# Long tiles: 2 to 4 key blocks of each unit's probabilities turned by DMA instead of by TensorE

## The reference, cut to what matters

```
x = x + attn(layernorm(x))        # 16 heads, key of 64 + 64 numbers a token, value of 128
x = x + ffn(layernorm(x))         # 16 experts of 176, the best 2 a token, and a shared one of 352

q = (h @ Wqa @ Wqb)               # 16 heads x (64 without, 64 with rotation)
c_kv, k_pe = split(h @ Wkva)      # 64 + 64 numbers a token, shared by all heads
scores = q_full . k_full * 128 ** -0.5, causal
probs  = softmax(scores)
out    = (probs @ v) @ Wo         # v = c_kv @ Wkvb[v part]
```

## Time and profile before

| | |
|---|---|
| median of 3 runs | 1752.13 us (1750.12 to 1752.58) |
| the profiled execution | 1753.84 us, its span 1752.0 us |
| PE busy | 1522.4 us (87%) |
| DVE busy | 1308.7 us (75%) |
| ACT busy | 1027.3 us (59%) |
| POOL busy | 990.5 us (57%) |
| transposes of probabilities on PE (L838) | 2304 |
| granted TensorE clock, mean | 0.971 |

### The profile page before, as it was taken

The page is one execution under the profiler, slowest core; times in us unless marked ns, Lnnn a source line. Parts: engine busy times, 40 slices in busy tenths (PEclk is TensorE's granted clock), DMA queues, the critical chain, the costliest instruction groups (busy, mean ns, idle before and its releaser), DMA issues.

```text
span 1752.0 us, 45002 instructions
## 1 busy us (share of the span) xinstructions
PE 1522.4 (87%) x16388; PEld 1092.0 (62%) x16389; DVE 1308.7 (75%) x2967; ACT 1027.3 (59%) x2342; POOL 990.5 (57%) x1597
## 2 busy tenths in 40 slices
PE   8777988989879999998799999987999999889990
PEld 2355666666646776666477766664676676666660
DVE  2676888888768778887687788776877888655556
ACT  1365656656546666666566666664666666556660
POOL 3156774436477667456776765567776443553440
PEclk9989999999999999999999999999999999999995
DMA  6236752221353332213534332135232311347418
GB/s 179 55 87 140 153 78 42 60 55 35 69 98 65 69 65 60 54 28 67 109 64 69 62 63 54 21 66 117 62 66 54 59 27 30 87 131 225 136 42 292
DMA packets 329877, 144.41 MB, mean 82 GB/s; under 512 B 277346, under 2 KB 320389, under 8 KB 329672
## 3 DMA queue, kind: packets, MB, share of 16 engines
q1 hardware_dynamic: 304592, 105.41, 30.1%
q10 hardware_dynamic: 18168, 19.41, 3.6%
q0 software_dynamic: 6912, 16.83, 3.0%
HBM read 47.04 MB, written 29.53 MB: 44 GB/s over the span
## 4 chain that ended last, share of the span: by engine, by line
PE 48%; DVE 26%; ACT 9%; issue 6%; DMA 4%; SPq 3%; POOL 1%; ACTq 0%; DVEq 0%; POOLq 0%
PE of_ps L677 20%; PE s_ps L677 16%; PE t_ps L838 10%; DVE pT L1609 7%; DVE smax L1580 3%; ACT pT L1024 3%; DVE smax L1584 2%; DVE smax L1562 1%; SPq L467 1%; ACT probs L1151 1%; DVE nmax L1588 1%; DVE nmax L1591 1%; ACT probs L1156 1%; ACT work L1024 1%; DVE work L1414 1%
## 5 line engine op out<-in xcount | busy, mean ns | idle before, releaser
L1609 DVE TENSOR_TENSOR pT<-t_ps,pT 128x512 f16<-128x512 f32 (+3 forms) x688 | 409.6, 598 | 194.3 <-ACT pT L1024 190.9
L677 PE MATMUL s_ps<-kT,qT 128*128 128x512 f16 (+3 forms) x2304 | 493.3, 329 | 11.3 <-DMA qT<-work 6.7
L1024 ACT CAST pT<-t_ps 128x512 f16<-128x512 f32 (+3 forms) x688 | 354.5, 515 | 233.6 <-PE t_ps L838 232.9
L838 PE MATMUL t_ps<-id,probs 128*128 128x128 f32 x2304 | 383.3, 281 | 71.2 <-DVE pT L1609 31.5
L838 PEld LDWEIGHTS t_ps<-id,probs 128*128 128x128 f32 x2304 | 258.8, 142 | 176.5 <-issue 91.6
L1151 ACT ACTIVATE probs<-s_ps,nmax,fac 128x640 f32<-128x640 f32 (+3 forms) x256 | 269.0, 1051 | 1.7 <-DVE nmax L1588 1.7
L677 PEld LDWEIGHTS s_ps<-kT,qT 128*128 128x128 f16 x2304 | 219.4, 99 | 79.5 <-DMA qT<-work 7.2
L677 PEld LDWEIGHTS of_ps<-ckv,pT 128*128 128x128 f16 x6912 | 240.6, 98 | 37.5 <-DVE o_sb L1443 7.6
L677 PE MATMUL of_ps<-ckv,pT 128*128 128x64 f16 x6912 | 257.9, 193 | 5.5 <-DVE o_sb L1443 5.2
L677 PE MATMUL of_ps<-weights,xT 128*128 128x512 f16 (+1 forms) x936 | 208.5, 361 | 59.8 <-ACT work L1024 30.5
L1887 POOL TENSOR_TENSOR os_<-o_sb,os_ 128x512 f16<-128x512 f32 x60 | 70.2, 1169 | 178.0 <-ACT os_ L1024 175.7
(11 more groups left out here) (224 smaller groups left out, 2472.3 us busy)
## 6 DMA issues: line engine op xcount, KB each, us to landing
wgu_sb<-wgu ACTq DMA_DIRECT2D x8, 704.0 KB, 4.3
work<-lists SPq DMA_DIRECT2D x40, 128.5 KB, 2.1
qT<-lists SPq DMA_DIRECT2D x40, 128.5 KB, 2.1
x_sb<-x SPq DMA_DIRECT2D x32, 128.0 KB, 2.4
x<-x SPq DMA_DIRECT2D x32, 128.0 KB, 2.4
dense<-den SPq DMA_DIRECT2D x32, 128.0 KB
weights<-dense ACTq DMA_DIRECT2D x1, 4096.0 KB, 20.0
qT<-y_exp SPq DMA_DIRECT2D x16, 256.0 KB, 6.6
```

What stands on the lines that cost most here:

```text
L677: return pe_.matmul(o, a, b, start=start, stop=stop)
L838: last = pe_.transpose(t_ps[:, h, c * P:(c + 1) * P], probs[:, u % 2, g * L + j * P:g * L + (j + 1) * P], id32[:, :])
L1024: return act.copy(o, i)
L1609: dve.tensor_tensor(pT[:, u % 2, 1, h, 0:w], t_ps[:, h, 0:w], pT[:, u % 2, 0, h, 0:w], ALU.subtract).then_inc(s.lo_p, 1)
```

## The change

In the four long tiles the first d = 2, 3, 3, 4 key blocks of a unit (i = 4, 5, 6, 7) are no longer turned by PE. ACT casts them from `probs` to a staging area that lies just ahead of `probs` (high part), DVE writes the low part over the start of `probs` itself, and one DMA transposes both, 2 d blocks, into `pT`. PE turns the other 3, 3, 4, 4 blocks, in one piece, through the bank u % 2 of `t_ps`. The number of ACT and DVE instructions for it stays two each a unit. `values` takes the PE part first.

New waits: the exponentials of unit k + 2 (and DVE's shifted write) wait until the DMA has read unit k; a DMA waits for DVE's low part and for the values of two units before; the values wait for the DMA. PE's turn waits for the low part of the last unit in the same bank, two units before. On ACT the order in iteration k becomes exps(k+1), prob_hi(k), staged_hi(k+1), on DVE the maxima of k+2, prob_lo(k), staged_lo(k+1).

On the SP queue a unit's transposition stands at the start of each iteration, and the other DMAs of a long tile are given places between them. The queries' transposition becomes four pieces of 8 blocks: two at the end of the tile, two after the first two units of the next (all four at its end for i = 7). The x2T, xT and store of tile 3 move into tile 4.

Also: the low part of the first output half of tile 1 goes ahead of the normalized rows on POOL, and its DMA ahead of keys and queries; `q0` of tile 2 moves from (1, 3) to (2, 0); the shared expert's result is added into `x1` and stored from there, without the buffer `den`.

```diff
+TURNED = [0, 0, 0, 0, 2, 3, 3, 4]
+def queries_in(n):
+    return 16 * sum(4 if m >= 2 and TURNED[(m - 2) % TB] else 1 for m in range(n % 2, n + 1, 2))
+def halves_by_pe():
+    uses, last = {}, {}
+    for t, u in units_in_order():
+        dma = TURNED[t % TB] > 0
+        for h in (1,) if dma else (0, 1):
+            bank = u % 2 if dma else h
+            uses[t, u, h] = (len(uses), bank, last.get(bank))
+            last[bank] = len(uses) - 1
+    return uses
...
-        probs = sb("probs", [P, 2, S], F32)
-        pT = sb("pT", [P, 2, 2, 2, 512], F16)
+        STAGE = 2 * P
+        probs_mem = sb("probs_mem", [P, 2, STAGE + S], F32)
+        probs = probs_mem[:, :, STAGE:]
+        pT = sb("pT", [P, 2, 2, 1024], F16)
...
+            def turn_query_part(n, part):
+                if part == 0:
+                    sp.wait_ge(s.rope_done, n + 1)
...
+                a, hs_ = part // 2, slice(part % 2 * 8, part % 2 * 8 + 8)
+                sp.dma_start_transpose(qT[:, n % 2, a, part % 2 * 8 * P:(part % 2 + 1) * 8 * P].rearrange("p (h n) -> p h n", n=P),
+                                       qs_of(n)[:, a, hs_, :].rearrange("p h d -> p (h d)")).then_inc(q_in[n % 2], 16)
+            def turn_probs(t, u):
+                g_ = unit_of(t, u)
+                sp.wait_ge(s.lo_s, DMA_UNIT[t, u] + 1)
+                sp.wait_ge(s.pv_made, g_ - 1)
+                d = TURNED[t % TB]
+                sp.dma_start_transpose(pT[:, u % 2, 0, 0:2 * d * P].rearrange("p (k n) -> p k n", n=P),
+                                       probs_mem[:, u % 2, :].bitcast(F16)[:, 2 * STAGE - d * P:2 * STAGE + d * P]).then_inc(p_in[u % 2], 16)
...
+            def long_section(t):
+                n, p, q, m = t + 2, t - 1, t - 2, t + 4
+                i = t % TB
+                for k in range(units(t)):
+                    turn_probs(t, k)
+                    if i == 4:
+                        if k == 0:
+                            turn_x2(p - 1)
+                        if k == 1 and has(m - 1):
+                            turn_x(m - 1)
+                        if k == 2:
+                            store_dense(q - 1)
+                    elif k < 2 and has(n - 1):
+                        turn_query_part(n - 1, k + 2)
+                    if k == 3:
+                        load_residual(p)
+                    if k == 4:
+                        turn_output(p, 1)
+                    if k == 5 and has(m + 1):
+                        load_x(m + 1)
+                    if k == 9:
+                        turn_hidden(q)
+                    if k == 12 and i < 7 and n % TB > 0 and has(n):
+                        turn_keys(n)
+                    if k == 13:
+                        turn_x2(p)
+                    if k == 14 and has(m):
+                        turn_x(m)
+                    if k == 14 and i == 7 and has(t + 1):
+                        turn_keys(t + 1)
+                        turn_keys(n)
+                    if k == 15:
+                        turn_output(t, 0)
+                        store_dense(q)
+                if has(n):
+                    for part in range(4 if i == 7 else 2):
+                        turn_query_part(n, part)
...
+            d = TURNED[i]
+            if d:
+                return [(0, j) for j in (range(d, i + 1) if h else range(d))]
...
                 pe_.wait_ge(s.exp_done, 2 * g_ + h + 1)
-                if g_ > 0:
-                    pe_.wait_ge(s.lo_p, 2 * (g_ - 1) + h + 1)
+                if before is not None:
+                    pe_.wait_ge(s.lo_p, before + 1)
...
-                for h in range(2):
-                    pe_.wait_ge(s.lo_p, 2 * g_ + h + 1)
+                order = (1, 0) if by_dma(t, u) else (0, 1)
+                for h in order:
+                    if (t, u, h) in PE_HALF:
+                        pe_.wait_ge(s.lo_p, PE_HALF[t, u, h][0] + 1)
+                    else:
+                        pe_.wait_ge(p_in[u % 2], 16 * (DMA_UNIT[t, u] // 2 + 1))
...
                 if h == 0:
                     act.wait_ge(s.max_ready, g_ + 1)
+                    staged_free(act, t, u)
...
+            def staged_hi(t, u):
+                act.wait_ge(s.exp_done, 2 * unit_of(t, u) + 2)
+                copy(staged(t, u, 0), probs[:, u % 2, 0:P * TURNED[t % TB]]).then_inc(s.hi_s, 1)
...
                     exps_ahead(t, k, 0)
                     prob_hi(t, k, 1)
+                    ahead = unit_of(t, k) + 1
+                    if ahead < len(UNIT_AT) and by_dma(*UNIT_AT[ahead]):
+                        staged_hi(*UNIT_AT[ahead])
...
+            def staged_lo(t, u):
+                dve.wait_ge(s.hi_s, DMA_UNIT[t, u] + 1)
+                dve.tensor_tensor(staged(t, u, 1), probs[:, u % 2, 0:P * TURNED[t % TB]], staged(t, u, 0),
+                                  ALU.subtract).then_inc(s.lo_s, 1)
```

More of the change, by code:

```diff
@@ L78, in shares_rope, with units_in_order, units_by_dma @@
     return n < 2 or n % TB in (2, 3)
+TURNED = [0, 0, 0, 0, 2, 3, 3, 4]
+def queries_in(n):
+    return 16 * sum(4 if m >= 2 and TURNED[(m - 2) % TB] else 1 for m in range(n % 2, n + 1, 2))
+def units_in_order():
+    return [(t, u) for t in range(NT) for u in range(units(t))]
+def halves_by_pe():
[7 more added lines that the diff above has]
+    return uses
+def units_by_dma():
+    out = {}
+    for t, u in units_in_order():
+        if TURNED[t % TB]:
+            out[t, u] = len(out)
+    return out
+PE_HALF = halves_by_pe()
+DMA_UNIT = units_by_dma()
+UNIT_AT = units_in_order()
 def shifted(i, u):
@@ L266, in build @@
         xin = [sem(f"x_in{k}") for k in range(XS)]
+        p_in = [sem(f"probs_in{k}") for k in range(2)]
         k_in = [sem(f"keys_in{k}") for k in range(KS)]
@@ L498, in section @@
                 n, p, q, m = t + 2, t - 1, t - 2, t + 4
-                i = t % TB if has(t) else None
+                i = t % TB
                 if has(q) and i == 0:
@@ L526, in section @@
-                if has(t) and i not in (0, 2, 3):
-                    turn_output(t, 0)
-                if has(q) and q < NT - 1 and (i is None or i >= 4):
-                    store_dense(q)
-                if i == TB - 1 and has(t + 1):
-                    turn_keys(t + 1)
-                if has(n) and i >= 4:
-                    if n % TB > 0:
-                        turn_keys(n)
-                    turn_queries(n)
-                if has(q) and i is not None and i < 4:
-                    store_dense(q)
+                if i < 3:
+                    if has(p):
+                        turn_x2(p)
+                    if has(m) and i != 0:
+                        turn_x(m)
+                    if has(q):
+                        store_dense(q)
@@ L549, in _ @@
             for t in range(NT):
-                section(t)
+                if TURNED[t % TB]:
+                    long_section(t)
+                else:
+                    section(t)
             def expert_rows(n, q):
@@ L649, in norm @@
                 st_.do(eng.tensor_tensor(y, y, u, ALU.mult))
+            if between is not None:
+                between()
             parts = []
@@ L880, in section @@
                     side(t, k, 0)
-                    turn(t, k, 0)
+                    turn(t, k, 1 if by_dma(t, k) else 0)
                     scores_ahead(t, k, 0)
                     side(t, k, 1)
-                    turn(t, k, 1)
+                    if not by_dma(t, k):
+                        turn(t, k, 1)
                     scores_ahead(t, k, 1)
@@ L1192, in section @@
                     side(t, k, 0)
-                    prob_hi(t, k, 0)
+                    if not by_dma(t, k):
+                        prob_hi(t, k, 0)
                     side(t, k, 1)
@@ L1713, in section @@
                     side(t, k, 0)
-                    prob_lo(t, k, 0)
+                    if not by_dma(t, k):
+                        prob_lo(t, k, 0)
                     side(t, k, 1)
@@ L1717, in section @@
                     prob_lo(t, k, 1)
+                    ahead = unit_of(t, k) + 1
+                    if ahead < len(UNIT_AT) and by_dma(*UNIT_AT[ahead]):
+                        staged_lo(*UNIT_AT[ahead])
                     if shifted(t % TB, k):
```

90 lines of the change are left out of this document (52 added, 38 removed).

## The result

The changed kernel takes 1841.69 us (median of 4 runs, 1834.98 to 1849.36) where the kernel before takes 1751.24 (4 runs, 1750.12 to 1752.58): ratio 1.052, 95% interval 1.048 to 1.056. It is slower by 5%, 59 us above the upper end of the range. Its profiled execution took 1842.84 us with a span of 1841.0.

A forecast was written before the change was run, and what follows sets the result against it. TensorE, busy 87% of the span, was taken to lead, but not alone. The terms -42 + 11 - 8 + 12 + 10 = -17 took 1752 to 1735 us; range 1702 to 1783, the forecast's own 1722 to 1747.

The forecast's parts named there:

- 1, turns off TensorE: Long tiles: 768 block turns leave TensorE, 0.11 us each, gaining only in units with products: -42 us, bounds 0 and -84.
- 2, copies unchanged: Long tiles' copies and subtractions: same number, VectorE's work unchanged within 0.01 us a unit, ScalarE's 0.03 more: 0.
- 3, the round trip: Bare units of long tiles: exponentials wait until the DMA has read the buffer two units before: +11 us, bounds 0 and +60.
- units that go free: Units with a product reset the trip, so the first one or two bare units after go free: +18 becomes +11 us.
- rival A: Bare units: the round trip binds and time goes up; with 0.7 us more a trip, 1780 us; chance 0.30.
- C: Rival, tiles 14 and 15: VectorE takes over, 25 of the 42 us not gained, 1760 us, likelier 1748 to 1750; chance 0.15.
- the +18: Longer round-trip periods over 8 bare units and 4 sequences, in us, before allowing for units that go free.
- 4, decoupling: Long tiles: turns wait for the low part two units before, not one, recovering a fifth of TensorE's other idle time: -8 us.
- 5, the SP queue: From tile to tile: the first unit's transposition starts about 2.5 us late, 1.5 of it slack: +12 us, bounds 0 and +40.
- 6, the crossing: From tile 7 of a sequence to tile 0 of the next: keys land 3.3 us later, three times: +10 us, at most +15.
- 7, "nothing": Store from x1, the second tile's low part sooner, one query product half a unit later, banks of turned halves: 0.
- The signs named: TensorE turns fall by 768, busy time by 60 to 84 us; 8 blocks land in about 3.1 us, 3.8 or more meaning A.

The follow-up runs named there:

- high_only: Changed kernel with VectorE's low parts of the staged blocks left out and only high blocks transposed by DMA (computation incomplete): 1722.7 us, ratio 0.984 to the kernel before.
- none_turned: Changed kernel with no key block turned by DMA, its SP order, query pieces and small parts kept: 1727.8 us, ratio 0.987 to the kernel before.
- own_keys_first: Changed kernel with 2, 2, 3, 4 blocks, low part beside probabilities (i = 4, 5), earlier keys and queries at sequence end, staged operations first: ratio 1.006 to before.
- The short rotation: GpSimd's rotation cut to one of 17 heads in 22 of 32 tiles, in both kernels: ratio 1.032 for the changed kernel, 0.994 for the kernel before.
- keys_first: Changed kernel with keys' turns ahead of unit 14's transposition and query pieces behind units 14 and 15, for i = 7 only: 1819.5 us, ratio 1.039 to before.

## Why the prediction was wrong, by its own steps

**1, turns off TensorE (-42): not seen by itself.** In high_only tiles with i = 4 to 6 are 31 us below none_turned (193.0 - 190.8, 210.5 - 201.7, 234.4 - 214.7). But VectorE has 104 us less to do there as well (1314.4 against 1210.1), so this is not the turns alone. With the computation whole (own_keys_first) the same tiles are 19 us above none_turned. The price was a little low: the earlier trace rows show 0.47 and 0.54 us for four turns, 0.12 to 0.14 a block, where the sum took 0.11.

**2, copies unchanged (0): this step failed.** The price from the earlier trace rows was right for an undisturbed subtraction (681 at 512 columns), but those four lay where nothing was in the way, and 256 new ones lie beside GpSimd's work, which fills 57% of the span. They took 763 ns on average, 55 us above undisturbed in all. The sentence "VectorE's work is unchanged" took a row's duration without its condition: the old subtraction read PSUM, the new one reads SBUF twice. The short rotation shows that half of these 55 us reached the end time almost one to one. VectorE at 78 to 84% of a tile was not idle enough to hide it.

**3, the round trip (+11, bounds 0 and +60): the main step that failed.** At its best the trip is what was worked out: in tile 15 two units take 6.28 us against 6.24, and 8 blocks land in 3.05 us against 3.15. The means are another matter. From the exponentials to the landing, a bare unit takes 6.3, 6.3, 7.0 and 7.4 us in tiles with i = 4 to 7, against 5.0, 5.4, 5.7 and 6.2: 1.2 longer (the trace has the landings of every second unit). The sum had every operation start when its input was there. The low part in fact waits for VectorE's turn (1.1 to 1.8 us on average from the high part's start, 0.6 to 0.75 at best), stalls, and then waits for the queue. And the products do not reset the trip, as the note on units that go free supposed: from exponentials to exponentials a unit with a product takes 0.5, 0.3, 0.1 and 0.1 us longer than before in tiles with i = 4 to 7. By rival A's rule, 6.4 us for each 0.1, the 1.2 make some 75 us, an estimate; the turns cost 114 in all, with the crossing and the units with products in it. So A had the right mechanism, with 0.7 where 1.2 was due. It binds most in the short ones of the long tiles: units 11 to 15 take 12.7 us in tile 12 where they took 9.7, and 13.6 in tile 15 where they took 14.1. A and C aren't separate here, since the trip passes through VectorE: of about 120 us some half hang on VectorE's own instructions. Redone from its own rows the trips of the shorter tiles come out at about 5.5, 5.3 and 4.7 us and not 5.7, 5.4 and 4.99; that takes some 6 us off the +18 and changes nothing here.

**4, decoupling (-8): not seen by itself.** No run isolates it.

**5, the SP queue (+12): too small.** In tiles with i = 5 to 7 the first two units waited mostly 2.9 to 4.5 us from their low part to the issue, where the prediction had the first 2.5 late and called 1.5 of that slack. What this costs in all was not isolated; none_turned shows that the same queue without the transpositions costs nothing.

**6, the crossing (+10, at most +15): failed in kind.** The keys cost 5 us each (19.6 us of waiting, 4.1 before), not far from 3.3. The queries were not in the sum: four pieces issued one after another behind the output's turn, 29 us more waiting than before (36.0 against 6.7). keys_first takes 24 us back. The three tiles with a crossing take 45 us more than before, tile 31 without one 4.1; so the crossing is some 11 us each, 33 in all, an estimate from these.

**7, "nothing" (0): failed, for the better.** It was worth -22 us. I looked at POOL's idle time, where the question was what stands behind the output's turn: ScalarE's write of `os_`, and TensorE behind that. The chain of waits of one tile with i = 2 would have shown it.

**The range.** The bounds of parts 3, 5 and 6 add to +115, which with part 1 in full reaches 1825; I took them as independent and cut at A. They were not: all three need the same VectorE and the same queue, and all came out high together. That this is why is argued; no run separates it. By the runs it was -22 for part 7 and about +114 for the turns.

**The signs named.** Turns by TensorE fell by 768, but its busy time only by 18 us against none_turned (1499.0 to 1481.2), where 60 to 84 were forecast. In high_only, with the same turns, it is 1429.9, 69 less. The granted clock goes with this (0.978 in none_turned, 0.944 in the changed kernel, 0.956 in high_only), and a turn took 288 ns where it took 281. The landing of 8 blocks was 3.1 us in the median, the sign for "not A", and A was nearest all the same: the sign looked at the transfer, where the loss was in front of it. The rule of the Trainium skill that was weighed ("VectorE: DVE Perf Modes", Rules for kernel authors: "Use TensorE if PSUM dest is OK; xbar DMA otherwise") came out right here. Its two figures are not the reason: four more blocks by DMA cost 0.64 us (2.41 to 3.05), and what made the trip too long lay mostly ahead of the transfer.

## What to carry to other kernels

Here a DMA that took work off the leading engine put a loop through every engine that prepares it. Price such a loop with each engine's present backlog, not with durations at rest, and look first at the engine that is second in the chain. When an operand moves from PSUM to SBUF, ask what else reads SBUF at the same time: here a subtraction with two SBUF inputs cost 2.6 us beside GpSimd instead of 0.4. And price each edit from the chain of its own tile: the two small ones were the whole gain.

## What the runs showed of the hardware

- A VectorE subtraction with two SBUF inputs stands until GpSimd's running instruction has ended, and can lose its turn to more than one (3.15 us at 611.8, across two): 412 ns undisturbed at 256 columns, 3165 at most; with one input in PSUM it never took over 693. Beside GpSimd's issues of indirect DMAs it mostly isn't held (10 of 13).
- A transposing DMA of SBUF to SBUF with 8 blocks of 128x128 (2 bytes) occupies SP's queue for 1.2 us, as long as one with 4; 32 blocks take 4.8. It lands in 2.4 us with 4 blocks, 2.7 with 6 and 3.05 with 8 at best. Of 27 that were issued within 0.5 us behind another transposition, 24 landed in 2.4 to 3.3 us and three in 4.4 to 4.7.
- The granted clock was lower where TensorE stood: 0.71 in 16 us of which it worked 7.0, and 1.00 in tiles 12 to 15 of the kernel before, of which it worked 93%.
